# Another order of work on all five engines in a decoder layer of three stages

## The reference

```
x = layernorm(x + attn(x))          # block A: 16 heads, chunks of 128 tokens, ternary weights
x = layernorm(x + xattn(x, ctx))    # block B: 32 query heads, 8 kv heads, window 64, ALiBi
x = layernorm(x + ffn(x))           # block C: dense 512x512 + top-2 of 8 low-rank experts

attn:  qkv, g = bitlinear(x); per token softmax over the 16 heads: softmax(q k^T) v,
       plus q @ kv_state of the chunk before; rmsnorm; bitlinear
xattn: q = [ctx, x] @ Wq;  keys and values of ctx and of x, both masked to 64 back;
       softmax(q k^T / 4 + alibi) v;  @ Wo
ffn:   x @ base_w^T + b + 2 * sum over the two best experts of gate * (x @ A_e) @ B_e
```

## Time and profile before

| what | us |
|---|---|
| median of 3 runs | 1010.35 |
| lowest, highest run | 1008.79, 1015.64 |
| the profiled execution, device time | 1009.06 |
| its span, first to last instruction | 1007.1 |
| a load of x_in, of ctx, a store of y, issue to landing | 4.3, 3.6, 3.0 |

### The profile page before, as it was taken

How to read it: one execution, slowest core, us unless ns; L and a number is a source line. 1 busy time by engine, 2 the same in 40 slices (tenths; PEclk the granted TensorE clock), 3 DMA queues, 4 the chain that set the end, 5 groups by cost and what they waited for, 6 DMA issues and landing times.

```text
span 1007.1 us, 22681 instructions
## 1 busy us (share of the span) xinstructions
PE 842.8 (84%) x10257; PEld 529.3 (53%) x10257; DVE 521.1 (52%) x1058; ACT 326.1 (32%) x420; POOL 85.3 (8%) x103
## 2 busy tenths in 40 slices
PE   4678578688998798988898899889987997889985
PEld 2345367345853485447644674458544853464342
DVE  4434535644584458543864477345844572316222
ACT  5142222253215421434234321532154313220520
POOL 1001101100200002000300021001100010010010
PEclk9899969999999999999999999999999998999998
DMA  8900100000001000100001000100000000000000
GB/s 314 218 30 22 42 2 2 22 22 2 2 2 43 22 2 2 43 22 2 2 23 42 2 2 1 49 17 2 1 22 23 2 1 22 1 1 1 22 1 21
DMA packets 18816, 27.08 MB, mean 27 GB/s; under 512 B 5401, under 2 KB 7577, under 8 KB 18721
## 3 DMA queue, kind: packets, MB, share of 16 engines
q1 hardware_dynamic: 18432, 24.84, 8.3%
q10 hardware_dynamic: 288, 0.80, 0.2%
HBM read 21.44 MB, written 4.19 MB: 25 GB/s over the span
## 4 chain that ended last, share of the span: by engine, by line
PE 59%; ACT 14%; DVE 14%; issue 6%; DMA 2%; SPq 2%; POOL 1%; ACTq 0%; POOLq 0%; DVEq 0%
ACT p_b L700 9%; PE ps L1024 7%; PE ps L947 6%; PE ps L1097 5%; PE ps L1058 5%; PE ps L930 4%; PE ps L989 4%; DVE max_b L1296 4%; PE ps L965 3%; SPq L462 2%; PE ps L1033 2%; PE ps L784 2%; PE ps L867 2%; PE ps L857 2%; PE ps L836 2%
## 5 line engine op out<-in xcount | busy, mean ns | idle before, releaser
L700 ACT ACTIVATE p_b<-ps 128x2048 f32<-128x2048 f32 x64 | 106.5, 1664 | 102.0 <-PE ps L1033 102.0
L1296 DVE TENSOR_REDUCE max_b<-ps 128x4 f32<-128x768 f32 (+2 forms) x160 | 105.8, 711 | 37.6 <-PE ps L1003 31.7
L1024 PE MATMUL ps<-q_b,k_b 32*128 32x512 f32 (+1 forms) x512 | 68.7, 607 | 29.0 <-ACT p_b L700 25.4
L1322 DVE STREAM_TRANSPOSE o_nat<-ps 128x512 f32<-128x512 f32 x32 | 21.0, 695 | 117.2 <-PE ps L1049 117.2
L989 PE MATMUL ps<-k_b,q_b 32*128 32x192 f32 (+2 forms) x1024 | 56.4, 334 | 20.0 <-DVE max_b L1296 14.8
L1097 PE MATMUL ps<-base_t,x_t 128*128 128x512 f32 x128 | 65.6, 641 | 1.8 <-ACT gm_t L713 0.9
L1196 DVE TENSOR_REDUCE max_a<-ps 128x8 f32<-128x1024 f32 x32 | 37.7, 1220 | 52.1 <-PE ps L836 52.1
L1049 PE MATMUL ps<-p_b,v_b 128*32 128x256 f32 (+1 forms) x1024 | 62.6, 362 | 2.0 <-ACT p_b L700 2.0
L930 PE MATMUL ps<-c_t,wq 128*128 128x256 f32 x256 | 62.0, 386 | 2.1 <-DVE out_a L1219 1.2
L1214 DVE STREAM_TRANSPOSE sum_a<-ps 128x512 f32<-128x512 f32 x16 | 11.5, 717 | 100.5 <-PE ps L870 90.9
L989 PEld LDWEIGHTS ps<-k_b,q_b 32*128 32x128 f32 x1024 | 39.2, 184 | 45.3 <-DVE max_b L1296 24.7
(11 more groups left out here) (184 smaller groups left out, 1453.7 us busy)
## 6 DMA issues: line engine op xcount, KB each, us to landing
x_in<-x SPq DMA_DIRECT2D x8, 512.0 KB, 4.3
p_b<-ctx SPq DMA_DIRECT2D x8, 512.0 KB, 3.6
y<-x SPq DMA_DIRECT2D x8, 512.0 KB, 3.0
p_b<-L_attn_qkv_w SPq DMA_DIRECT2D x3, 1024.0 KB, 7.1
p_b<-L_xattn_Wq SPq DMA_DIRECT2D x1, 2048.0 KB, 10.8
p_b<-L_attn_proj_w SPq DMA_DIRECT2D x1, 1024.0 KB, 5.4
p_b<-L_ffn_base_w SPq DMA_DIRECT2D x1, 1024.0 KB, 10.7
wo<-L_xattn_Wo SPq DMA_DIRECT2D x8, 128.0 KB, 9.3
```

Of the source, the lines that this page charges most:

```text
L700: act.activation(p_b[:, j % 2, :, 0:cols], ps[:, 4:8, 0:cols], ACT.Exp, scale=DB ** -0.5).then_inc(pb_here.sem, 1)
L1024: pe.matmul(bank(4 + r)[:, 0:nb * P], k_b[strip[r], half, 2 * j:2 * j + 2, :, :].rearrange("p c s k -> p (c s k)"), q_b[strip[r], 2 * j:2 ...
L1296: ins = dve.tensor_reduce(max_b[:, half, 0, i:i + k, 2 * n:2 * n + 2], ps[:, 4 + 2 * n:6 + 2 * n, :].rearrange("p r (i n) -> p i r n", i=2 ...
```

## The change

The lists of all engines are put in another order. Every stage of TensorE's list is in both, with the same splits, and so are those of VectorE, ScalarE and GpSimd. The point at which the list is cut into steps moves: b3_s(0) to b3_s(4) and b3_w(0) to b3_w(2) now belong to the end of the step, with lag B in place of C_. SyncE's store gets the new lag D_ = 3 and the loop one step more. The diff without its context lines:

```diff
--- before.py
+++ after.py
@@ -393,7 +393,7 @@
-        NEXT, A, B, C_ = -1, 0, 1, 2
+        NEXT, A, B, C_, D_ = -1, 0, 1, 2, 3
@@ -406,7 +406,7 @@
-            for i in range(-1, NB + 2):
+            for i in range(-1, NB + 3):
@@ -487,7 +487,7 @@
-            run(sp, [(NEXT, a0), (A, b1), (C_, c2)], late)
+            run(sp, [(B, b1), (A, a0), (D_, c2)], late)
@@ -549,7 +549,7 @@
-            run(pool, [(B, a4), (C_, b4), (A, a3), (C_, c1), (NEXT, a0), (NEXT, a1), (C_, c2)])
+            run(pool, [(NEXT, a0), (A, a4), (C_, c2), (B, b4), (NEXT, a1), (NEXT, a3), (B, c1)])
@@ -714,12 +714,12 @@
-            run(act, [(C_, of(b3, 2)), (C_, of(b3, 3)), (C_, of(b3, 4)), (C_, of(b3, 5)), (C_, of(b3, 6)), (C_, of(b3, 7)), (B, of(b1_k, 0)),
-                      (B, of(b1_qc, 1)), (A, a1_q), (A, a1_state), (A, a1_v), (A, of(a2_m, 0)), (A, of(a2_x, 0)), (A, b1_mix),
-                      (C_, of(b4_x2, 0)), (C_, of(b4_x2, 1)), (B, of(a4, 0)), (B, of(a4, 1)), (B, of(b1_x1, 0)), (B, of(b1_x1, 1)),
-                      (A, of(a3_sq, 0)), (B, b1_v), (A, of(a2_m, 1)), (B, of(b1_k, 1)), (A, of(a2_x, 1)), (A, of(b1_c, 0)), (A, of(b1_c, 1)),
-                      (A, of(a3_sq, 1)), (C_, of(c1_x2, 0)), (C_, of(c1_x2, 1)), (C_, c1), (A, of(b1_qc, 0)), (A, b1_kc), (A, a3_t),
-                      (C_, c2), (B, of(b2, 0)), (NEXT, a1), (B, of(b2, 1)), (B, of(b3, 0)), (B, of(b3, 1)), (C_, c2_y)], late)
+            run(act, [(A, a1_q), (A, a1_state), (A, a1_v), (C_, of(b4_x2, 0)), (C_, of(b4_x2, 1)), (B, of(a4, 0)), (B, of(a4, 1)),
+                      (A, of(a2_m, 0)), (B, of(b1_x1, 0)), (B, of(b1_x1, 1)), (A, of(a2_x, 0)), (B, b1_v), (B, of(b1_k, 1)), (A, b1_mix),
+                      (A, of(a2_m, 1)), (A, of(b1_c, 0)), (A, of(b1_c, 1)), (A, of(a3_sq, 0)), (A, of(a2_x, 1)), (A, of(a3_sq, 1)),
+                      (C_, of(c1_x2, 0)), (A, of(b1_qc, 0)), (C_, of(c1_x2, 1)), (B, of(b2, 0)), (C_, c1), (A, b1_kc), (A, a3_t), (C_, c2),
+                      (B, of(b2, 1)), (NEXT, a1), (B, of(b3, 0)), (B, of(b3, 1)), (B, of(b3, 2)), (B, of(b3, 3)), (B, of(b3, 4)),
+                      (B, of(b3, 5)), (B, of(b3, 6)), (B, of(b3, 7)), (C_, c2_y), (A, of(b1_qc, 1)), (A, of(b1_k, 0))], late)
@@ -1101,21 +1101,21 @@
-            run(pe, [(C_, of(b3_s, 0)), (A, of(a1_qkv, 1, [0])), (C_, of(b3_s, 1)), (A, of(a1_qkv, 1, [1])), (C_, of(b3_w, 0)),
-                     (C_, of(b3_s, 2)), (A, of(a1_qkv, 1, [2])), (C_, of(b3_w, 1)), (C_, of(b3_s, 3)), (C_, of(b3_w, 2)), (C_, of(b3_s, 4)),
-                     (C_, of(b3_w, 3)), (B, of(b1_qc, 1, range(2))), (C_, of(b3_s, 5)), (C_, of(b3_w, 4)), (C_, of(b3_s, 6)),
-                     (C_, of(b3_w, 5)), (C_, of(b3_s, 7)), (C_, of(b3_w, 6)), (C_, of(b3_w, 7)), (B, of(b1_qc, 1, range(2, KT))),
-                     (A, a1_qt), (A, a1_state), (A, of(a1_v, 0)), (C_, of(b4, 0, 0)), (A, of(a1_v, 1)), (C_, of(b4, 0, 1)),
-                     (A, of(a2_s, 0, range(HT))), (C_, of(b4, 1, 0)), (C_, of(b4, 1, 1)), (A, of(a2_m, 0)), (A, of(a2_x, 0, range(HT))),
-                     (A, of(a2_v, 0)), (B, of(b1_x1, 0)), (B, of(b1_x1, 1)), (B, of(b1_v, range(2))), (A, of(a2_s, 1, range(HT))),
-                     (B, of(b1_q, 1, range(2))), (B, of(b1_v, range(2, KB))), (A, of(a2_m, 1)), (B, b1_k), (A, of(a2_x, 1, range(HT))),
-                     (A, of(b1_c, 0)), (B, of(b1_q, 0, range(2))), (A, of(a2_v, 1)), (A, a2_rec), (A, of(b1_c, 1)),
-                     (B, of(b1_q, 0, range(2, KT))), (B, of(b1_q, 1, range(2, KT))), (C_, of(c1_x2, 0)), (B, of(b2, 0, 0)),
-                     (C_, of(c1_x2, 1)), (A, of(b1_qc, 0, range(2))), (B, of(b2, 0, 1)), (C_, of(c1, 0)), (C_, of(c1, 1)),
-                     (A, of(b1_qc, 0, range(2, KT))), (B, of(b2, 0, 2)), (A, b1_kc), (A, a3_t), (B, of(b2, 0, 3)), (C_, c2_gates),
-                     (A, of(a3, 0)), (C_, of(c2, 0, 0)), (B, of(b2_max, 0)), (A, of(a3, 1)), (B, of(b2, 1, 0)), (NEXT, a1),
-                     (B, of(b2, 1, 1)), (C_, of(c2, 0, 1)), (B, of(b2, 1, 2)), (NEXT, of(a1_qkv, 0, [0])), (C_, of(c2, 1, 0)),
-                     (B, of(b2, 1, 3)), (NEXT, of(a1_qkv, 0, [1])), (C_, of(c2, 1, 1)), (B, of(b2_max, 1)), (NEXT, of(a1_qkv, 0, [2]))], late)
+            run(pe, [(A, of(a1_qkv, 1, [0])), (C_, of(b3_w, 3)), (C_, of(b3_s, 5)), (C_, of(b3_w, 4)), (A, of(a1_qkv, 1, [1])),
+                     (C_, of(b3_s, 6)), (C_, of(b3_w, 5)), (A, of(a1_qkv, 1, [2])), (C_, of(b3_s, 7)), (C_, of(b3_w, 6)), (C_, of(b3_w, 7)),
+                     (B, of(b1_qc, 1, range(2))), (B, of(b1_qc, 1, range(2, KT))), (A, a1_qt), (C_, of(b4, 0, 0)), (A, a1_state),
+                     (C_, of(b4, 1, 0)), (A, of(a1_v, 0)), (C_, of(b4, 0, 1)), (C_, of(b4, 1, 1)), (A, of(a1_v, 1)),
+                     (A, of(a2_s, 0, range(HT))), (B, of(b1_x1, 0)), (A, of(a2_m, 0)), (B, of(b1_x1, 1)), (A, of(a2_x, 0, range(HT))),
+                     (B, of(b1_q, 0, range(2))), (B, of(b1_q, 0, range(2, KT))), (A, of(a2_v, 0)), (B, of(b1_v, range(2))),
+                     (B, of(b1_v, range(2, KB))), (A, of(a2_s, 1, range(HT))), (B, b1_k), (B, of(b1_q, 1, range(2))), (A, of(a2_m, 1)),
+                     (A, of(b1_c, 0)), (B, of(b1_q, 1, range(2, KT))), (A, of(b1_c, 1)), (B, of(b2, 0, 0)), (A, of(a2_x, 1, range(HT))),
+                     (B, of(b2, 0, 1)), (A, of(a2_v, 1)), (B, of(b2, 0, 2)), (A, a2_rec), (A, of(b1_qc, 0, range(2))), (B, of(b2, 0, 3)),
+                     (C_, of(c1_x2, 0)), (A, of(b1_qc, 0, range(2, KT))), (C_, of(c1_x2, 1)), (B, of(b2_max, 0)), (C_, of(c1, 0)),
+                     (B, of(b2, 1, 0)), (C_, of(c1, 1)), (B, of(b2, 1, 1)), (A, b1_kc), (A, a3_t), (B, of(b2, 1, 2)), (A, of(a3, 0)),
+                     (C_, c2_gates), (C_, of(c2, 0, 0)), (B, of(b2, 1, 3)), (C_, of(c2, 0, 1)), (A, of(a3, 1)), (B, of(b2_max, 1)),
+                     (C_, of(c2, 1, 0)), (NEXT, a1), (B, of(b3_s, 0)), (C_, of(c2, 1, 1)), (NEXT, of(a1_qkv, 0, [0])), (B, of(b3_s, 1)),
+                     (B, of(b3_w, 0)), (NEXT, of(a1_qkv, 0, [1])), (B, of(b3_s, 2)), (NEXT, of(a1_qkv, 0, [2])), (B, of(b3_w, 1)),
+                     (B, of(b3_s, 3)), (B, of(b3_w, 2)), (B, of(b3_s, 4))], late)
@@ -1413,20 +1413,20 @@
-            run(dve, [(A, of(a1_t8, 1, (0,))), (NEXT, a0), (A, of(a1_t8, 1, (1,))), (C_, of(b3_on, 0)), (C_, of(b3, 1)), (C_, of(b3_on, 1)),
-                      (C_, of(b3_of, 0)), (C_, of(b3_of, 1)), (A, of(a1_t8, 1, (2,))), (A, of(a2_max, 0)), (C_, of(b4_z, 0)),
-                      (C_, of(b4, 0)), (C_, of(b4_z, 1)), (C_, of(b4, 1)), (C_, of(b4, 2)), (C_, b4_x2), (A, of(a2_out, 0, 0)),
-                      (A, of(a2_out, 0, 1)), (A, of(a2_max, 1)), (A, of(a2_out, 1, 0)), (A, of(a2_out, 1, 1)), (A, a2_rec), (B, of(b1_q, 0)),
-                      (A, a3_ms), (B, of(b1_q, 1)), (A, of(a3, 0)), (B, of(b2, 0, 0, 0)), (B, of(b2, 0, 0, 1)), (A, of(a3, 1)),
-                      (B, of(b2, 0, 1, 0)), (B, of(b2, 0, 1, 1)), (C_, c1), (A, a3_round), (C_, of(c1_top, 0)), (C_, of(c1_top, 1)),
-                      (B, of(b2, 0, 2, 0)), (B, of(b2, 0, 2, 1)), (C_, of(c1_top, 2)), (B, of(b2, 0, 3, 0)), (B, of(b2, 0, 3, 1)),
-                      (B, of(b2_max, 0)), (A, of(a3_z, 0)), (NEXT, a0_round), (A, of(a4_stats, 0)), (A, of(a3_z, 1)), (B, of(b2, 1, 0, 0)),
-                      (B, of(b2, 1, 0, 1)), (B, of(b2, 1, 1, 0)), (B, of(b2, 1, 1, 1)), (A, of(a4_stats, 1)), (C_, of(c2_z, 0)),
-                      (B, of(b2, 1, 2, 0)), (B, of(b2, 1, 2, 1)), (NEXT, of(a1_nat, 0, (0,))), (B, of(b2, 1, 3, 0)), (B, of(b2, 1, 3, 1)),
-                      (B, of(b2_max, 1)), (A, of(a4_stats, 2)), (NEXT, of(a1_nat, 0, (1,))), (C_, of(c2, 0)), (C_, of(c2_z, 1)),
-                      (C_, of(c2, 1)), (NEXT, of(a1_t8, 0, (0,))), (NEXT, of(a1_nat, 0, (2,))), (C_, of(c2, 2)), (NEXT, of(a1_t8, 0, (1,))),
-                      (C_, c2_y), (NEXT, of(a1_nat, 1, (0,))), (NEXT, of(a1_t8, 0, (2,))), (A, a4), (NEXT, of(a1_nat, 1, (1,))),
-                      (NEXT, of(a1_nat, 1, (2,))), (B, of(b3, 0))])
+            run(dve, [(C_, of(b4, 0)), (C_, of(b4_z, 1)), (C_, of(b4, 1)), (C_, of(b4, 2)), (C_, b4_x2), (B, a4), (A, of(a2_max, 0)),
+                      (B, of(b1_q, 0)), (A, of(a2_out, 0, 0)), (A, of(a2_out, 0, 1)), (A, of(a2_max, 1)), (B, of(b1_q, 1)), (NEXT, a0),
+                      (B, of(b2, 0, 0, 0)), (B, of(b2, 0, 0, 1)), (B, of(b2, 0, 1, 0)), (B, of(b2, 0, 1, 1)), (A, of(a2_out, 1, 0)),
+                      (A, of(a2_out, 1, 1)), (B, of(b2, 0, 2, 0)), (B, of(b2, 0, 2, 1)), (A, a2_rec), (B, of(b2, 0, 3, 0)),
+                      (B, of(b2, 0, 3, 1)), (A, a3_ms), (B, of(b2_max, 0)), (A, of(a3, 0)), (A, of(a3, 1)), (B, of(b2, 1, 0, 0)),
+                      (B, of(b2, 1, 0, 1)), (C_, c1), (A, a3_round), (C_, of(c1_top, 0)), (B, of(b2, 1, 1, 0)), (B, of(b2, 1, 1, 1)),
+                      (C_, of(c1_top, 1)), (C_, of(c1_top, 2)), (B, of(b2, 1, 2, 0)), (B, of(b2, 1, 2, 1)), (A, of(a3_z, 0)),
```

(7 more changed lines are left out.)

## The result

The changed kernel takes 1026.99 us (median of four executions, 1025.60 to 1032.23) where the kernel before took 1013.00 on the same chip (four, 1008.79 to 1016.37): a ratio of 1.015, 95% interval 1.0091 to 1.0208. It is slower. The forecast was 996, with 983 to 1009 as its range, so both the sign and the range were wrong. The profiled execution took 1027.5, its span is 1025.4.

A forecast was written before the change was run, and what follows sets the result against it. TensorE was taken as the bound, busy 842.8 of 1007.1 us. Six steps -11.4, start -5.2 and clock +2.7 gave -13.9: 1009.06 to 995.2 for a profiled execution, so 996 was predicted, range 983 to 1009.

The forecast's parts named there:

- Parts 1 to 3: Per step: tile-shape changes -1.2 us, b3 scores and value products -2.5, stretch from value products to b1_v -0.9.
- the 104.3 of the sum: Sign of a right forecast: middle steps of 104.3 us, 105.6 with a drop of the clock.
- Part 1: TensorE's changes of tile shape, fewer in the new order: 1.2 us less a step, bounds 0.5 and 1.3.
- Part 4: Row-maxima (b2) stretch: waits of 6.2 against 3.5 us, 2.7 us more a step, bounds 1.0 and 6.0.
- rival (a): VectorE becomes the bound in the b2 stretch: +5.2 us a step, 1027, priced at 1016; chance 0.13.
- part 5: Start and end: start 5.2 us less (bounds -2 and -8), other queues nothing, end 0 (bounds -3 and +4).
- Part 6: TensorE's clock: one drop in each of six steps, 7.8 us, less 5.1 paid now: +2.7, bounds -5 and +10.
- Rival (b): One more clock drop a step than charged, sparse places b1_x1 and b2: 6 x 1.3 = 8 us, 1004; chance 0.15.
- (c): Saved shape changes and b3 gaps are taken up by waits behind them, only the start gained: 1005; chance 0.15.
- (d): The b2 stretch costs nothing, as before: 2.7 x 6 = 16 us better, 980; chance 0.12.

The follow-up runs named there:

- the missing corner: The changed kernel with GpSimd's list alone rewritten (x_res and base bias adds moved), no matmul added: 1001.14 us, ratio 0.9904 to the kernel before.
- the one of 985.93 us: The changed kernel with GpSimd's list rewritten and 5, 11 and 6 unread matmuls put into TensorE's waits: 985.93 us, ratio 0.9753 to the kernel before.

## Why the prediction was wrong, step by step

**Parts 1 to 3 held, as far as they can be read.** The waits that were to go went (L1024, L867, L816), and the step without the two disturbances is 103.95 us, 0.35 from the 104.3 of the sum, or 0.6 the other way with L1364 as before. The one term that can be read by itself, the wait at b1_x1(0), was 3.2 in the walk, 2.7 with VectorE not held, and 3.7 with it. Part 1, the changes of tile shape, has no wait of its own, and no run separates it from the rest.

**Part 4** was called the weakest term, and as a walk it held: b2(1,2) was put at 0.8 us and is at most 0.6 where nothing is held, with no matmul added too (the missing corner). In the kernel as changed it is 2.6. The 2.0 between them are what L1364 and L1173 lose, 1.05 and 1.14 us, ahead of the reduction. I had looked for the danger in how much VectorE has to do there (rival (a)), not in how long a given instruction of it takes.

**The sentence that failed** is the one in part 5 on the other queues: "GpSimd adds proj_bias earlier [...] nothing." I weighed the move only by the transfer that it lets go, x(b+1). The durations of VectorE's instructions were taken from the trace of before and carried to their new places as if they were fixed. They are fixed only as long as the same thing of GpSimd runs beside them. The trace of before held the warning: L1364 took 1.10 us there and its like in size 0.17, and I didn't ask why. With the clock held all that is held costs 106.84 - 103.95 = 2.9 us a middle step, 15.4 in all six (637.9 against 622.5 us); up to 0.9 of it, L1364, the kernel before paid as well.

That sentence is about x_res, beside which L1271 is held. For the other pair of adds, the base bias (L545), beside which L1364 and L1173 are held, the prediction has no term at all. That pair follows GpSimd's scaling L531 in both lists; it is VectorE that now comes to it earlier. Before:

```profile
591.93 1.36 POOL L531 TENSOR_SCALAR nat<-out_a,st_a 128x512 f32<-128x512 f32 x2 [4.92 <-DVE st_a L1248]
592.27 1.82 DVE L1296 TENSOR_REDUCE max_b<-ps 128x4 f32<-128x768 f32 x2 [0.45 <-PE ps L1003]
593.25 2.49 POOL L545 TENSOR_TENSOR x<-x,base_bias 128x512 f32<-128x512 f32 x2
594.68 1.10 DVE L1364 TENSOR_TENSOR g_c<-g_c,gs_c 128x16 f32<-128x16 f32 x1
595.70 0.68 DVE L1173 TENSOR_SCALAR xq<-nat 128x1024 bf16<-128x1024 f32 x1
```

There L1364 begins 1.43 us after the pair and L1173 as the pair ends. After, the reduction between is b2(1,0)'s of 1.15 us, L1364 begins 0.07 us after the pair and L1173 as its second add does.

The Trainium skill has this rule: "SBUF — State Buffer", section Who interferes with whom, says that GpSimd and VectorE share one pair of ports, that it is taken for a whole instruction and the other engine stands still for so long, that VectorE's instructions with two operands in SBUF and the two-port forms of a plain scalar operation take it, and that reductions don't. The trace agrees on each: held were L1364, L1271, L1386 and L1387 (two operands in SBUF) and L1173 (fp32 to bf16, within SBUF); the reduction L1385 was not. That L1173 runs in a two-port form is the page's reading, no run here shows it alone.

**Part 6, the clock, was mis-sized.** I charged one drop of 1.3 us a step, priced by drops that last 3.4 us. Without the remedies there are two, and together they last three or four times as long, 10 to 14 us of a step at 1.2 GHz, and holding the clock brings 110.1 - 106.3 = 3.8 us a step, although the matmuls for it take part of that again. Why one drop became two follows from the first error: the two waits behind which the clock falls are the two that VectorE's held instructions lengthen, and with VectorE free (the missing corner) the drop at b2(1,2) is gone, while the one at b1_x1(0), still a wait of 2.7 us, stays. Rival (b), one more drop a step, had the mechanism and too small a price: it gave 1004. In the kernel before no drop came in three of six steps, not four: the first of the six, of 105.99 us, also has a clock of 0.97. The section that I quoted beside it (the Trainium skill, "TensorE: Matmul & The Clock Gate", section HAM oscillation) tells of waits longer than the 2.1 us of the kernel before, so those three steps don't contradict it, as I had said; in the changed kernel, with waits of 2.6 and 3.7 us, the drops do come in every step.

**Part 5, the start.** It was to bring 5.2 us. L816 of the first step did start 3.4 earlier (54.58 instead of 57.95), but the second rounding comes at 169.37 us instead of 168.46. That is 6 us off, and held instructions are hardly a part of it: L1173 takes 0.69 us at both roundings, and VectorE's busy time is 40.8 us between them in this kernel and in the one of 985.93 us alike, and only 0.8 us more ahead of the first. The sum of this part (-2.1 + 0.7 - 3.8) also leaves out the 1.7 us that its text gives to a0. The rest I didn't settle. The time to the second rounding is 174.6 to 177.9 us in the kernels of this study where 27 us or more between the first two roundings run at 1.2 GHz, and 166.5 to 169.4 where 17 or fewer do (the changed kernel too); what decides between the two isn't shown.

**The sum.** Against the 995.2 of the forecast for a profiled execution: a middle step is 4.5 us longer than the 105.6 with its one drop, six times 27; the start 6 longer, the end 1 shorter; 995.2 + 27 + 6 - 1 = 1027, which is what was measured. Of the 4.5, by the means of the table, the clock is 110.1 - 106.3 = 3.8 less the 1.3 charged, the held instructions are 106.3 - 103.7 = 2.6, and the walk -0.6: 4.5. The split hangs on the order of the remedies: with GpSimd's list first, it has 4.6 and the clock 1.8 less the 1.3.

**Other rivals.** (a) VectorE bound in the b2 stretch: the 1027 of its whole sum (I priced it at 1016) is the measured time by luck, since the sum comes another way. Waits on max_b are 3.7 us a step, not above 6; of its signs only the mean clock under 0.94 came (0.938). (c) savings absorbed: refuted, the savings are there at 103.95. (d) b2 costs nothing: only near true with VectorE free.

## What to carry to other kernels

When an order of work is changed, the durations from the old trace are good only beside the same neighbours. Before moving a GpSimd instruction, list what VectorE does in its time: a subtraction of 16 columns beside an add of 512 took as long as the add (1.22 us). Where VectorE's chain feeds TensorE, put GpSimd's long instructions beside VectorE's reductions out of PSUM, which took the same 1.82 us there. And a kernel whose TensorE has waits of 2 to 4 us must be costed with the clock behind each of them: a few matmuls that nobody reads, put into such a wait, were worth 17 us of 1027 here.

## What was not expected of the hardware

- A VectorE product of 128x2 elements takes 0.16 us alone and 1.21 beside a GpSimd add of 128x512, an operation on 128x16 0.17 and up to 1.22. In the timelines shown each ended within 0.1 us of the GpSimd add beside it.
- The rounding L1173 takes 0.68 us alone and 1.82 where it began about when GpSimd's second add of 1.24 us did: close to the sum of the two.
- 22 to 30 unread matmuls a step made the kernel faster in both lists of GpSimd, by 15 and by 17 us; eight and four of them in the kernel before, by some 7.
- The time from the start to the second rounding moved by up to 11 us between the profiled kernels, by 6.7 between two that differ in GpSimd's list alone, with the share of it at 1.2 GHz. The whole time of one kernel varies as much from run to run (993.6 to 1005.5 us in four), so the list need not be the cause. This wasn't pursued.
